# Weighting ahead of the scores in each half step of self attention, in a fused decoder layer

## The reference

```
x = x + self_attention(layernorm(x))
x = x + cross_attention(layernorm(x), ctx, ctx)
x = x + experts(layernorm(x))       # one shared, 16 routed, 2 per token
```

```
a1 = softmax(q1 @ k1.T * scale) @ v ;  a2 = softmax(q2 @ k2.T * scale) @ v
o  = a1 - lam * a2 ;  o = rms_norm(o) * subln_w * (1 - lambda_init)
x  = x + concat(o) @ W_proj + b_proj
```

## Time and profile before

| | us |
|---|---|
| median of 3 runs (593.27 to 596.82) | 595.57 |
| the profiled execution | 595.6 |
| its span | 594.4 |
| TensorE busy | 541.0 (91%) |
| VectorE busy | 311.4 (52%) |
| ScalarE busy | 261.2 (44%) |
| GpSimd busy | 229.5 (39%) |

### The profile page before, as it was taken

How to read it: one execution, slowest core, us unless ns; L and a number is a source line. 1 busy time by engine, 2 the same in 40 slices (tenths; PEclk the granted TensorE clock), 3 DMA queues, 4 the chain that set the end, 5 groups by cost and what they waited for, 6 DMA issues and landing times.

```text
span 594.4 us, 10885 instructions
## 1 busy us (share of the span) xinstructions
PE 541.0 (91%) x3792; PEld 372.6 (63%) x3792; DVE 311.4 (52%) x677; ACT 261.2 (44%) x420; POOL 229.5 (39%) x473
## 2 busy tenths in 40 slices
PE   8968879689887879899999899999999999999888
PEld 6544435355544544665685457456999999999347
DVE  5867865957796797896242752111222222222184
ACT  6326555444562554835412200201666666665110
POOL 2534775635553554422010004563243334443100
PEclk9989998989897999999999989999999999999899
DMA  7892562713222141990029906222233333332552
GB/s 241 230 204 74 152 193 78 229 53 112 81 67 74 42 145 59 150 285 1 0 71 350 288 0 195 90 89 71 73 91 94 95 93 96 91 90 76 198 187 72
DMA packets 62197, 72.46 MB, mean 122 GB/s; under 512 B 14816, under 2 KB 55264, under 8 KB 60608
## 3 DMA queue, kind: packets, MB, share of 16 engines
q1 hardware_dynamic: 58160, 60.59, 36.0%
q0 software_dynamic: 3792, 10.39, 5.0%
q10 hardware_dynamic: 192, 0.79, 0.6%
HBM read 45.32 MB, written 26.03 MB: 120 GB/s over the span
## 4 chain that ended last, share of the span: by engine, by line
PE 49%; issue 18%; DVE 13%; POOL 10%; DMA 5%; ACT 3%; SPq 2%; POOLq 0%; DVEq 0%; ACTq 0%
PE ps L612 17%; PE ps L623 9%; POOL y_rows L1632 7%; DVE nmax L875 3%; PE ps L539 3%; PE ps L440 2%; PE ps L376 2%; PE ps L389 2%; PE ps L428 2%; DVE OT L882 2%; PE ps L407 2%; PE ps L505 2%; PE ps L520 2%; POOL goes_to L1626 1%; PE ps L632 1%
## 5 line engine op out<-in xcount | busy, mean ns | idle before, releaser
L875 DVE TENSOR_REDUCE nmax<-ps 128x8 f32<-128x1024 f32 x64 | 77.7, 1215 | 43.4 <-PE ps L407 39.4
L668 PE MATMUL ps<-xt,Wn 128*128 128x128 f32 x752 | 91.8, 275 | 0.3 <-ACT xt L1450 0.3
L668 PEld LDWEIGHTS ps<-xt,Wn 128*128 128x128 f32 x752 | 87.7, 192 | 0.6 <-ACT xt L1450 0.5
L1348 ACT ACTIVATE prob<-ps 128x1024 f32<-128x1024 f32 x64 | 65.5, 1023 | 35.9 <-PE ps L428 35.9
L1632 POOL DMA_INDIRECT y_rows<-yo,goes_to x47 | 46.0, 978 | 81.8 <-DVE yo L1129 81.5
L1443 ACT ACTIVATE sil<-ps 128x512 f32<-128x512 f32 x32 | 19.1, 597 | 122.1 <-PE ps L612 119.3
L1121 DVE TENSOR_TENSOR ht<-sa,ps 128x256 f32<-128x256 f32 x47 | 19.8, 421 | 99.2 <-PE ps L679 95.2
L612 PE MATMUL ps<-xT,W1s 128*128 128x512 f32 x128 | 63.7, 622 | 3.5 <-DVE yo L1129 1.9
L623 PE MATMUL ps<-W3s,hTs 128*128 128x256 f32 x256 | 56.5, 381 | 4.4 <-DVE hTs L1052 4.4
L612 PE MATMUL ps<-xT,W2s 128*128 128x512 f32 x128 | 60.3, 593 | 0.0
L1052 DVE TENSOR_TENSOR hTs<-sil,ps 128x512 f32<-128x512 f32 x32 | 21.9, 686 | 70.1 <-PE ps L612 66.0
(11 more groups left out here) (186 smaller groups left out, 854.6 us busy)
## 6 DMA issues: line engine op xcount, KB each, us to landing
W<-in_L_ffn_routed_w_dram SPq DMA_DIRECT2D x12, 1024.0 KB
pack_q<-qk_parts SPq DMA_DIRECT2D x48, 128.0 KB, 3.1
xg<-x_slots SPq DMA_DIRECT2D x47, 129.0 KB
x_slots<-zero SPq DMA_DIRECT2D x11, 512.0 KB, 10.3
pack_k<-qk_parts SPq DMA_DIRECT2D x42, 128.0 KB, 3.1
qk_parts<-part SPq DMA_DIRECT2D x21, 256.0 KB, 3.1
yg<-y_rows SPq DMA_DIRECT2D x4, 1024.0 KB, 8.6
X<-in_x_dram SPq DMA_DIRECT2D x4, 512.0 KB, 7.0
```

Source lines behind the costliest of these rows:

```text
L668: r = t.matmul(ps[:, 2 + p, h * P:(h + 1) * P], Wn[:, n % 3, k, h * P:(h + 1) * P], xt[:, p, k, :], start=(k == 0), stop=(k == KT - 1))
L875: v.tensor_reduce(nmax[:, s % 4, a, :, :], ps[:, b:b + 2, :].rearrange("p m (h t) -> p m h t", h=4), AX_X, ALU.max, negate=True).then_inc( ...
L1348: a.activation(prob[:, n:n + 2, :], ps[:, 2:4, :], ACT.Exp, scale=HD ** -0.5).then_inc(exped, 1)
```

## The change

In each half step TensorE's `pv` is issued directly behind `exps`, and `scores` of three steps on behind it. Before, it was `exps`, `scores`, `pv`. Nothing else changes: the waits travel with their functions, and the other engines' lists stay as they are.

```diff
             for s in range(STEPS):
                 exps(s, 0)
+                if s:
+                    pv(s - 1, 1)
                 if s + LEAD < STEPS:
                     scores(s + LEAD, 0)
-                if s:
-                    pv(s - 1, 1)
                 between(s, 0)
                 exps(s, 1)
+                pv(s, 0)
                 if s + LEAD < STEPS:
                     scores(s + LEAD, 1)
-                pv(s, 0)
                 if s + LEAD - 1 < STEPS:
                     turn_max(s + LEAD - 1)
                 between(s, 1)
```

## The result

The changed kernel is slower: 609.38 us (median of 4 runs, 606.60 to 612.99) against 594.42 for the kernel before, ratio 1.0267 with an interval of 1.0175 to 1.036. Measured once more beside the kernel before, it was 611.3 against 592.95, ratio 1.0285 (1.0226 to 1.0344). So the loss is 15 to 18 us. The forecast said slower, 603.3 us, range 598 to 609.

A forecast was written before the change was run, and what follows sets the result against it. No engine was taken as full: TensorE leads, with about 30 us of waits in the half steps. Losses by stretches of steps summed to 7.7 us, added to 595.6 for 603.3 us, range 598 to 609.

The forecast's parts named there:

- the sum: Losses of the half steps added by stretches of steps: 7.7 us in all, onto 595.6 us, giving 603.3 us.
- (a): First half of a step: scores at e + 0.90 instead of e + 0.23, second half's weighting not before e + 3.37.
- (b): Second half: scores queue behind the waiting weighting; without filler TensorE is through 1.0 us later, with 1.9 us filler nothing waits.
- 14 to 16: Steps 14 to 16: maximum 0.7 us later with VectorE's and GpSimd's chain, step 16 0.4: 1.1 us.
- 24 to 28: Steps 24 to 28: VectorE runs without a gap, step 27's second maximum comes 1.0 us later: 1.0 us.
- (c): Tiling changes on TensorE: leaving row-split products costs about 0.10, once per half step before, twice after; about 1.4 us in all.
- the prediction's own last sign of being wrong: Forecast is wrong if added stretches of half clock carry more than the waits.
- Clock: Rival, chance 0.17: longer waits bring two or three more falls of TensorE's clock at 1.7 us each: 607.5 us.
- Covered: Rival, chance 0.14: DMA and VectorE waits swallow the quiet steps' losses, tiling changes alone stay: 597.0, up to 598.5 us.
- Faster: Rival, chance 0.05: the weighting fills TensorE's waits for the maximum in first halves, saving 2.8 us: 592.8 us.
- e + 1.9: Weighting's place in a quiet step, from the exponential's products at e; the transposition must end before it for a gain.
- scores ahead of a waiting weighting: Rival, chance 0.02: TensorE's queue runs the scores ahead of the waiting weighting after all, time stays at 595.6 us.

The follow-up runs named there:

- first_half: Against the kernel before, only first half steps issue the weighting ahead of the scores; second halves keep the old order: 599.2 us, ratio 1.0104.
- all_kept_active: Changed kernel plus unneeded unit-matrix transpositions on TensorE in the quiet steps, step 16 and the waits for DMAs and VectorE: 596.4 us, 1.0048 to the kernel before.
- before_kept_active: Kernel before plus unneeded unit-matrix transpositions on TensorE in three waits, two for DMAs and one for VectorE (steps 6, 11, 21): 589.9 us, ratio 0.9927.
- kept_active: Changed kernel plus 5 to 10 unneeded unit-matrix transpositions on TensorE in each of nine quiet steps, ahead of the weighting: 605.1 us, 1.0201 to the kernel before.
- transpose_first: Changed kernel with VectorE's transposition of the weighted values ahead of a step's first maximum instead of behind it: 598.8 us, 1.0076 to the kernel before.

## Why the prediction was wrong

The direction, the wait and its place were right; the size was not, 15 to 18 us for 7.7, because a second mechanism was left out of the sum.

*(a) and (b), the order.* Right to a few hundredths of a microsecond, as step 9 shows, and by first_half shown to run over VectorE's transposition. The terms of the sum can be compared in the two traces whose waits are filled. From the starts of the exponential's products in all_kept_active and before_kept_active, the changed order lost, in us, by the prediction's stretches:

| steps | predicted | measured | |
|---|---|---|---|
| 0 to 2 | 1.5 | 1.51 | |
| 3 to 6 | 0.2 | 0.20 | a DMA ends last in step 7, as said |
| 7, 8 | 0.4 | 0.42 | |
| 9 to 11 | 0.8 | 0.47 | |
| 12, 13 | 0.4 | 0.42 | |
| 14 to 16 | 1.1 | -0.41 | 1.2 of clock in the kernel compared with (L390 above, 3.19 for 1.99) |
| 17, 18 | 0.7 | 0.76 | |
| 19 to 21 | 0.7 | 0.79 | |
| 22, 23 | 0.9 | 2.51 | eight products at half clock, 3.44 for 1.99 |
| 24 to 28 | 1.0 | 4.41 | 0.7 up to step 28, then half clock from 225.7 to 232.5 |
| 29, 30 | none | -0.64 | |

With the three places of half clock left out (1.2 added to steps 14 to 16, 1.45 taken from steps 22 and 23, step 28 not counted), the terms add up to 7.2 for 7.7, and to 6.5 with steps 29 and 30. What was wrong in them is which half steps are safe: step 16 has a filler in its first half, yet its weighting waited 1.82 us (the row at 156.40), as VectorE came late to its maximum.

*(c), the tiling change.* The amount was right, 0.1 for a busy half step, the account wasn't. The prediction took entering the row-split products for free, because weighting to scores takes as long as weighting to projection. But both change the tiling. By the single products of step 8, going from row-split to weighting or filler costs 0.09 (0.15 from start to start, against 0.05 within), and going to row-split 0.09 too (0.33 against 0.24 behind a weighting, 0.31 against 0.22 behind a filler). Before, a half step with a filler had three such changes, now it has four. The Trainium skill says that changing the tiling mode drains TensorE (TensorEngine Tiling (Array Packing), Key Properties). The trace agrees, in every direction that it has, and not in one only as the prediction says.

*The clock.* Here the prediction failed. The step: "In the quiet steps 24 to 28 the clock stayed full, so a wait of 0.9 us by itself doesn't bring it down", from which two or three more falls at 1.7 us were made a rival with 0.17, and the sum took the clock as it was: no term at all. But (b) of the same prediction made the waits in just those steps longer (1.83 us in step 24), and what a wait of 0.9 does says nothing of them. The length of a wait was too thin a sign anyway. Before, this wait of 1.25 us stood in the same stretch, at full clock:

```profile
216.42 0.40 PE L407 MATMUL ps<-pack_k,pack_q 48*128 48x128 bf16 x8 [1.25 <-DVE nmax L875]
```

After, a wait of 1.33 us in step 2 (to 63.43) had a fall behind it, and waits of 1.27 us in step 9 and 1.82 in step 16 had none. The size in runs: 2 x (1 - clock) x time is the time at half clock, 28.5 us before (0.976) and 51 after (0.958). Of these 22.5 us more, 15 to 18 less 6.5, or 8 to 12 us, came through. The line of the table says 8.7 for the 0.019 of clock between the two. So the term that the sum had at nothing measured 8 to 12 us, at least as much as the order itself (6.5 to 7.8), which is the prediction's own last sign of being wrong. The page TensorE: Matmul & The Clock Gate of the Trainium skill (Terms) puts the penalty at about the time at the low clock multiplied by the share of pulses left out, by which an estimate here is 11 us; the runs lie near it.

*The rivals.* Clock (607.5) was nearest, and its mechanism is shown by kept_active, where filling the new waits brings the clock from 0.958 to 0.976 and the time down by 4 to 6 us. It isn't instead of the forecast's waits but stands on them. Covered is out by the table above. Faster is out: the waits for the maximum were filled, 6.5 to 0.9 us, and it bought nothing, as the transposition was never ready at e + 1.9. Even with the edit of transpose_first it is no gain. No row shows scores ahead of a waiting weighting.

*Still open.* Which exact waits bring the clock down. The changed kernel's two traces agree in steps 2, 24 and 26, but the mean clock of its other executions goes from 0.950 to 0.966, so the falls aren't the same in all. How the loss splits between busy and quiet steps is open too.

## What to carry to other kernels

Moving an operation forward on one engine moves whatever the others queue behind its old neighbour; follow the loop over all engines, and if an early product is wanted, move its consumer with it (transpose_first took back 11 to 13 us of the 15 to 18). On TensorE price a new wait twice, once for its length and once for the products at half clock that may follow it. Compare kernels at equal mean clock, and look where in the trace the falls lie, as a mean doesn't tell. Where a wait can't be removed, work that nobody reads may be worth its place.

## What was not expected of the hardware

Most of what one kernel's runs on one chip differ by goes with the granted clock: transpose_first took 592.3 us at 0.986 and 600.9 at 0.963, 3.7 us for each hundredth. Fifty-three transpositions of the unit matrix put into three waits made the kernel before 4.7 us faster, by raising the clock from 0.976 to 0.988. Waits of TensorE of the same length had a fall of the clock behind them or none: 1.33 us with one, 1.82 us without, in one trace. Each change between row-split, column-split and full products cost 0.09 us, whichever way it went.
